# LayerNorm stage of an attention and expert layer: normalising, transposing and copying tile j one tile later, behind the statistics of tile j+1

## The reference

```python
def _layernorm(x, axis=-1, eps=1e-5):
    m = jnp.mean(x, axis=axis, keepdims=True)
    v = jnp.var(x, axis=axis, keepdims=True)
    return (x - m) / jnp.sqrt(v + eps)

xn = _layernorm(x, axis=-1)
x = x + _L0_attn_ref(xn, wq, wkv_a, wkv_b, wo) + _L0_ffn_ref(xn, router_w, gate_w, up_w, down_w)
```

## Time and profile before

| | us |
|---|---|
| two timed executions | 7805.26 and 8367.38, median 8086.32 |
| the profiled execution | 7799.47 |
| its span, slowest core (core 1) | 7797.8 |
| spans of the other cores | 7779.5 to 7793.0 |
| VectorE busy | 2535.1 |
| TensorE busy | 5965.9 |
| ScalarE busy | 818.7 |

### The profile page before, as it was taken

How to read it: one execution, slowest core, us unless ns; L and a number is a source line. 1 busy time by engine, 2 the same in 40 slices (tenths; PEclk the granted TensorE clock), 3 DMA queues, 4 the chain that set the end, 5 groups by cost and what they waited for, 6 DMA issues and landing times.

```text
span 7797.8 us, 77136 instructions; the slowest of 8 cores (7779.5 to 7797.8 us)
## 1 busy us (share of the span) xinstructions
PE 5965.9 (77%) x28992; PEld 2783.4 (36%) x28992; DVE 2535.1 (33%) x4501; ACT 818.7 (10%) x1975; POOL 341.8 (4%) x377
## 2 busy tenths in 40 slices
PE   2655575556555655589999999999999999999900
PEld 1223232223222332234444444444444444444400
DVE  5433343334333433323312332123312332123244
ACT  2011211121111111100000000000000000000000
POOL 0000000000000000000000000000000000000000
PEclk9756575657565756599999999999999999999955
DMA  4200030003000300053243333333243332433166
GB/s 100 28 7 9 7 106 7 9 7 106 7 9 7 105 7 9 1 130 38 28 49 38 38 38 33 44 39 39 27 48 42 39 39 29 49 38 38 24 262 242
DMA packets 509816, 374.91 MB, mean 48 GB/s; under 512 B 468880, under 2 KB 470928, under 8 KB 486928
## 3 DMA queue, kind: packets, MB, share of 16 engines
q0 software_dynamic: 490336, 233.66, 22.4%
q1 hardware_dynamic: 19120, 136.32, 4.5%
HBM read 457.83 MB, written 83.89 MB: 69 GB/s over the span
## 4 chain that ended last, share of the span: by engine, by line
PE 74%; DVE 9%; issue 5%; DMA 4%; DVEq 4%; ACT 3%; ACTq 2%; POOL 0%; POOLq 0%; SPq 0%
PE psG L886 17%; PE psD L909 17%; PE psU L892 17%; PE psA L627 4%; PE psAV L609 4%; PE psA L634 3%; PE psA L555 3%; DMA rb<-scr 3%; PE psTa L600 2%; ACT probs L811 2%; DVEq L713 2%; DVE probsT L734 2%; PE psAV L660 2%; DVE colM L711 2%; PE psA L545 2%
## 5 line engine op out<-in xcount | busy, mean ns | idle before, releaser
L886 PE MATMUL psG<-xnT,gb 128*128 128x512 bf16 x6144 | 1391.5, 380 | 19.4 <-DMA ub<-uw 19.4
L892 PE MATMUL psU<-xnT,ub 128*128 128x512 bf16 x6144 | 1388.7, 379 | 0.0
L909 PE MATMUL psD<-db,hT 128*128 128x512 bf16 x6144 | 1328.6, 379 | 16.6 <-DVE hT L947 16.6
L947 DVE TENSOR_TENSOR hT<-sgt,psU 128x512 bf16<-128x512 f32 x384 | 264.0, 688 | 2409.5 <-PE psU L892 2409.5
L961 DVE SCALAR_TENSOR_TENSOR acc<-psD,comb,acc 128x512 bf16<-128x512 f32 x960 | 720.9, 751 | 541.4 <-PE psD L909 541.4
L886 PEld LDWEIGHTS psG<-xnT,gb 128*128 128x128 bf16 x6144 | 601.7, 98 | 746.7 <-issue 23.5
L909 PEld LDWEIGHTS psD<-db,hT 128*128 128x128 bf16 x6144 | 597.7, 97 | 747.5 <-issue 197.2
L892 PEld LDWEIGHTS psU<-xnT,ub 128*128 128x128 bf16 x6144 | 601.2, 98 | 724.9
L627 PE MATMUL psA<-kns,qn 128*128 128x512 bf16 (+3 forms) x640 | 309.3, 525 | 706.9 <-ACT probs L811 568.8
L934 ACT ACTIVATE sgt<-psG 128x512 f32<-128x512 f32 x384 | 229.4, 597 | 3676.5 <-PE psG L886 3676.5
L811 ACT ACTIVATE probs<-psA,colD 128x512 bf16<-128x512 f32 (+3 forms) x640 | 392.1, 620 | 1669.4 <-DVE colD L714 1475.0
(11 more groups left out here) (135 smaller groups left out, 2842.3 us busy)
## 6 DMA issues: line engine op xcount, KB each, us to landing
scr<-stage SPq DMA_DIRECT2D x64, 1024.0 KB, 3.9
gb<-gw POOLq DMA_DIRECT2D x96, 512.0 KB, 6.5
ub<-uw POOLq DMA_DIRECT2D x96, 512.0 KB, 8.3
db<-dw POOLq DMA_DIRECT2D x16, 3072.0 KB, 20.3
rb<-scr SPq DMA_DIRECT2D x32, 1024.0 KB, 11.7
rb<-scr POOLq DMA_DIRECT2D x32, 1024.0 KB, 10.9
xbuf<-x SPq DMA_DIRECT2D x16, 1024.0 KB, 5.9
xf<-x SPq DMA_DIRECT2D x16, 1024.0 KB, 15.1
```

Of the source, the lines that this page charges most:

```text
L886: i = t.matmul(ps_g[:], gb[sl][:, dc * 128:(dc + 1) * 128], xnt(dc)[:, tb * 512:(tb + 1) * 512], start=(dc == 0), stop=(dc == ND - 1))
L892: i = t.matmul(ps_u[:], ub[sl][:, dc * 128:(dc + 1) * 128], xnt(dc)[:, tb * 512:(tb + 1) * 512], start=(dc == 0), stop=(dc == ND - 1))
L909: i = t.matmul(ps_d[:], hT[:, fc * 2048 + tc * 128: fc * 2048 + (tc + 1) * 128], db[:, fc * 2048 + dcol * 512: fc * 2048 + (dcol + 1) * 51 ...
```

## The change

VectorE's loop is cut into three pieces. The first holds the statistics (L201 to L214) of tile tc. The second, `emit_xnb(j)`, is the wait for `rstd`, the negation and xnb, and marks `xn` and `lnused`. The third, `emit_evac(j)`, is the two copies. In the loop the statistics of tile tc come first, then `emit_xnb(tc - 1)` and `emit_evac(tc - 1)`; behind the loop stand those of the last tile. So that two tiles' values can be kept at once, the columns colC, colD and colE are replaced by pairs in a new tensor `lnc` (mean in columns 0 and 1, variance in 2 and 3, rstd in 4 and 5). One drain goes, that behind the mean of squares. ScalarE's order is kept, with the new columns. SyncE, GpSimd and TensorE have the same programs as before, and `xbuf`, `xnb` and the PSUM tiles have as many buffers as before.

```diff
@@ -123,6 +123,7 @@
                 ivf = EP(nc.sbuf_tensor("ivf", [32, 1], F32))
                 frq = EP(nc.sbuf_tensor("frq", [32, 2048], F32))
                 kfb = EP(nc.sbuf_tensor("kfb", [32, 2048], F32))
+                lnc = EP(nc.sbuf_tensor("lnc", [128, 8], F32))
                 psT0 = EP(nc.psum_tensor("psT0", [128, 1024], BF16))
                 psT1 = EP(nc.psum_tensor("psT1", [128, 1024], BF16))
 
@@ -195,46 +196,59 @@
                     v.drain()
                     VE.inc(i, 1)
                     mark(("cosarg",), VE)
+                    def emit_xnb(j):
+                        wait(v, ("rstd", j))
+                        v.tensor_scalar(out=lnc[:, j % 2:j % 2 + 1], in0=lnc[:, j % 2:j % 2 + 1],
+                                        scalar1=-1.0, scalar2=None, op0=ALU.mult)
+                        v.drain()
+                        i = v.tensor_scalar(out=xnb[:], in0=xbuf[j % 2][:],
+                                            scalar1=lnc[:, j % 2:j % 2 + 1],
+                                            scalar2=lnc[:, 4 + j % 2:5 + j % 2],
+                                            op0=ALU.add, op1=ALU.mult)
+                        v.drain()
+                        VE.inc(i, 1)
+                        mark(("xn", j), VE)
+                        mark(("lnused", j), VE)
+
+                    def emit_evac(j):
+                        for half in range(2):
+                            pt = psT0 if half == 0 else psT1
+                            wait(v, ("xpose", j, half))
+                            dst = xnT[:, half * 8 * 2048: half * 8 * 2048 + 8 * 2048].rearrange(
+                                "p (dc c) -> p dc c", c=2048)[:, :, j * 128:j * 128 + 128]
+                            src = pt[:].rearrange("p (j c) -> p j c", c=128)
+                            i = v.tensor_copy(dst, src)
+                            VE.inc(i, 1)
+                            mark(("xnTevac", j, half), VE)
+
                     for tc in range(NT):
                         wait(v, ("xload", tc))
                         xb = xbuf[tc % 2]
                         v.reduce_sum(colA[:], xb[:], axis=AX.X)
                         v.drain()
-                        v.tensor_scalar(out=colC[:], in0=colA[:], scalar1=float(1.0 / D),
-                                        scalar2=None, op0=ALU.mult)
+                        v.tensor_scalar(out=lnc[:, tc % 2:tc % 2 + 1], in0=colA[:],
+                                        scalar1=float(1.0 / D), scalar2=None, op0=ALU.mult)
                         v.drain()
                         wait(v, ("sq", tc))
-                        v.tensor_scalar(out=colD[:], in0=colB[:], scalar1=float(1.0 / D),
-                                        scalar2=None, op0=ALU.mult)
-                        v.drain()
-                        v.tensor_tensor(out=colA[:], in0=colC[:], in1=colC[:], op=ALU.mult)
-                        v.drain()
-                        v.tensor_tensor(out=colD[:], in0=colD[:], in1=colA[:], op=ALU.subtract)
-                        v.drain()
-                        i = v.tensor_scalar(out=colD[:], in0=colD[:], scalar1=LN_EPS,
+                        v.tensor_scalar(out=lnc[:, 2 + tc % 2:3 + tc % 2], in0=colB[:],
+                                        scalar1=float(1.0 / D), scalar2=None, op0=ALU.mult)
+                        v.tensor_tensor(out=colA[:], in0=lnc[:, tc % 2:tc % 2 + 1],
+                                        in1=lnc[:, tc % 2:tc % 2 + 1], op=ALU.mult)
+                        v.drain()
+                        v.tensor_tensor(out=lnc[:, 2 + tc % 2:3 + tc % 2],
+                                        in0=lnc[:, 2 + tc % 2:3 + tc % 2], in1=colA[:], op=ALU.subtract)
+                        v.drain()
+                        i = v.tensor_scalar(out=lnc[:, 2 + tc % 2:3 + tc % 2],
+                                            in0=lnc[:, 2 + tc % 2:3 + tc % 2], scalar1=LN_EPS,
                                             scalar2=None, op0=ALU.add)
                         v.drain()
                         VE.inc(i, 1)
                         mark(("var", tc), VE)
-                        wait(v, ("rstd", tc))
-                        v.tensor_scalar(out=colC[:], in0=colC[:], scalar1=-1.0,
-                                        scalar2=None, op0=ALU.mult)
-                        v.drain()
-                        i = v.tensor_scalar(out=xnb[:], in0=xb[:], scalar1=colC[:],
-                                            scalar2=colE[:], op0=ALU.add, op1=ALU.mult)
-                        v.drain()
-                        VE.inc(i, 1)
-                        mark(("xn", tc), VE)
-                        mark(("lnused", tc), VE)
-                        for half in range(2):
-                            pt = psT0 if half == 0 else psT1
-                            wait(v, ("xpose", tc, half))
-                            dst = xnT[:, half * 8 * 2048: half * 8 * 2048 + 8 * 2048].rearrange(
-                                "p (dc c) -> p dc c", c=2048)[:, :, tc * 128:tc * 128 + 128]
-                            src = pt[:].rearrange("p (j c) -> p j c", c=128)
-                            i = v.tensor_copy(dst, src)
-                            VE.inc(i, 1)
-                            mark(("xnTevac", tc, half), VE)
+                        if tc >= 1:
+                            emit_xnb(tc - 1)
+                            emit_evac(tc - 1)
+                    emit_xnb(NT - 1)
+                    emit_evac(NT - 1)
 
                 @block.scalar
                 def _(s):
@@ -246,9 +260,10 @@
                         SE.inc(i, 1)
                         mark(("sq", tc), SE)
                         wait(s, ("var", tc))
-                        s.activation(colE[:], colD[:], AF.Ln)
+                        s.activation(lnc[:, 4 + tc % 2:5 + tc % 2], lnc[:, 2 + tc % 2:3 + tc % 2], AF.Ln)
                         s.drain()
-                        i = s.activation(colE[:], colE[:], AF.Exp, scale=-0.5)
+                        i = s.activation(lnc[:, 4 + tc % 2:5 + tc % 2],
+                                         lnc[:, 4 + tc % 2:5 + tc % 2], AF.Exp, scale=-0.5)
                         s.drain()
                         SE.inc(i, 1)
                         mark(("rstd", tc), SE)
```

## The result

| | before | changed |
|---|---|---|
| timed executions | 22, from 7799.16 to 8684.66 us | 23, from 7820.10 to 8641.32 us |
| their median | 7969.36 us | 7939.64 us |
| profiled execution | 7799.47 us | 7823.30 us |
| mean span of the eight cores in it | 7787.5 us | 7813.4 us |
| first key/value matmul, mean of the eight cores | 182.2 us | 202.6 us |

Executions of one and the same program are up to 11% apart here, because in many of them the cores of one die or of both run at a lower clock; the two medians depend on how many of those each kernel drew, and every ratio here leaves them out. The ratio of changed to before is 1.0038, with a 95% interval of 1.0022 to 1.0054: the changed kernel is slower, by 17 to 42 us. The lowest executions of the two kernels are 20.9 us apart. By the bound of 2% the verdict is no change.

The account below looks back on a forecast made before the run. VectorE was taken to bound the LayerNorm stage, whose length goes to the end time. 7799.5 us plus 32.2, mainly from exposed x loads, gave 7831.7, say 7832 us (0.4% more); range 7814 to 7856.

Parts of the forecast that it names:

- the base of the sum: Whole kernel: starting time of 7799.5 us, the profiled execution before (span 7797.8 and 1.7 around it).
- terms of the stage: LayerNorm stage: savings, exposed load, start and end together issue the kvab load 32.2 us later than before.
- The wait for rstd: VectorE before the negation: the wait for ScalarE's Ln and Exp goes, 0.82 us becomes about 0.30, saving 0.52 a tile.
- The drain: VectorE behind the mean of squares: starts 0.08 us apart instead of 0.23, saving 0.15 us, possibly 0.
- The transposes' wait stays: VectorE before the first copy: the 1.37 us wait for TensorE's transposes stays in full.
- The late load: Load of tile j+2, issued behind xnb(j), has 2.83 us but lands after 5.9; pass 11.15 us against 8.58.
- The first pass gains: Start of the LayerNorm stage: one overlapped pass gains 2.5 us, reduce(2) at 36.2 against 38.71.
- The tail: End of the LayerNorm stage: last copy ends at 193.6 us against 159.82 and holds the kvab load, issued at 194.2.
- Every later stage unchanged: Behind the kvab issue: its transfer and every later stage stay unchanged, and nothing of them could start earlier.
- that x loads stay hidden: Rival, LayerNorm stage: loads stay hidden, pass 7.91 us, kvab issued 13 us earlier, 7787 us in total; chance 0.04.
- The longer landing: Rival, x loads: landing takes 9.9 us in every pass, a loss of 88 us, 7888 us in total; chance 0.05.
- The clock: Rival, later stages: TensorE's granted clock shifts, bounded at 6 us; chance 0.10 that later stages move the total over 15 us.

Follow-up runs that it names:

- the late load alone: Kernel before, only SyncE's wait changed: the load of tile tc waits for xnb(tc-1) instead of xnb(tc-2); ratio 1.0035, first matmul at 215.4 us.

## Why the prediction was right or wrong

**The time was wrong.** The measured median is 7939.64 us, and the range ended at 7856. The step that failed is the base of the sum, 7799.5 us from the profiled execution, with the sentence behind it: "The profiled one stands by the lower, and so does this forecast; it is not made against the median". The two executions shown were 7% apart, and I took the higher as something to set aside; the range of 42 us was then built from terms of the stage, and gave 6 us to the spread of executions. What the runs showed in its place: the kernel before has a median of 7969.36 us over 22 executions, 170 us over that base, and the changed one 7939.64 over 23, of which eight are below 7830 us and nine above 8000. No term of the sum stood for that. A forecast of a median has to say how many executions it expects near each of the two values it was shown, and its range has to follow from that.

**That the ratio came out is partly luck.** Against the profiled execution, 7823.30, the forecast of 7832 is 9 us off; as a ratio it was 1.0041, and 1.0038 was measured. But the terms of the stage summed to 32.2 us, and the first matmul moved by 20.4. Of the difference, 5.4 us came from later stages, where the forecast had nothing and where another run shows as much with nothing changed; and the interval of the ratio, 17 to 42 us, holds 20 as well as 32.

**The direction and the mechanism were right.** Point by point:

- *The wait for rstd.* Forecast: 0.30 us from the last statistic to the negation; measured 48.92 to 49.24, 0.32. Right.
- *The drain.* Forecast 0.08 us between the two starts; measured 48.39 to 48.46, 0.07. Right. Reduce to end of xnb: 5.08 us forecast, 5.08 measured (45.73 to 50.81).
- *The transposes' wait stays.* 1.37 us, right.
- *The late load.* Right in kind, and shown by two runs from both sides: three buffers take the loss away, the late load alone makes it. *Its size was the mis-sized term of the stage.* I took a landing of 5.9 us, core 1's median before; on core 3, the slowest after, it was

```profile
DMA to landing us min/median/max: 4.9/5.0/8.9
```

  5.0 us, and 5.0 on core 1 too. The pass shown above is 5.08 + 0.08 + 4.9 + 0.09 = 10.15 (xnb ends at 50.81, issue at 50.89, landing 4.9 later, reduce at 55.88), against a forecast of 11.15. Over 13 passes that would be 13 us. Some passes were longer, up to 11.3 us around 110 us, and the mean pass from tile 2 to tile 15 was (169.96 - 35.55) / 13 = 10.34, so the 13 passes came out 10.5 us shorter than forecast. I held a waiting time fixed that the change itself moved: waiting for a load changes when it is issued, and with that what it meets.
- *The first pass gains.* reduce(2) forecast at 36.2, measured at 35.55 on this core and 36.3 on core 2. Right.
- *The tail.* From the last reduce to the last copy 12.4 us forecast, 12.55 measured. kvab held by the copy, with some 0.6 us of GpSimd's start: 182.51 to 183.20. Right. The transfer itself was forecast at core 1's old 19.9 us; on core 3 it took 18.2 from issue to landing, but on core 3 it had taken 18.8 before, so most of the 1.7 us is a difference of the cores. The rest is open. As a mean of the cores the first matmul is 20.4 us later than before; on this core 20.7.
- *"Every later stage unchanged".* Not shown, and not refuted. The mean span grew by 25.9 us, 5.4 more than the first matmul moved, but the kernel before with a third buffer shows 5.9 us of the same kind with an unmoved stage. Forecast at 32.2, the difference of the spans came out at 25.9.

The rivals: that x loads stay hidden was out after the first look at the waits; but with a third buffer its forecast (7.91 us a pass, 13 us less) is what that kernel did, 7.91 and 12.5. So its arithmetic was right and its condition false. The longer landing didn't come, the opposite did. The clock moved nothing that could be told: 0.93 against 0.94 in the projection, 0.826 as a mean in both, and a part of the chain that ended last of 17% for each of the expert lines as in the earlier trace rows:

```profile
PE psD L924 17%; PE psG L901 17%; PE psU L907 17%; PE psA L642 4%; PE psAV L624 4%; PE psA L649 3%; PE psA L570 3%; DMA rb<-scr 3%; PE psTa L615 2%; PE psAV L675 2%; ACT probs L826 2%; DVEq L728 2%; DVE probsT L749 2%; DVE colM L726 2%; PE 
```

The prediction sets the fit of the Trainium skill ("DMA: Bandwidth & Descriptors", Anatomy of one DMA) against the trace. The page gives that fit for transfers issued from GpSimd. The x loads are issued from SyncE, so their 5.9 us neither bears it out nor refutes it.

## What to carry to other kernels

Before a piece of a loop is moved one iteration later, look for every buffer that it is the last reader of: it keeps that buffer one piece longer, and what refills it is late by as much. Here two buffers were enough with 11.3 us between issue and need, nearly always enough with 6.5, and not with 2.83, at 5 to 6 us of transfer; one more buffer, or releasing the buffer first and doing the statistics of the next tile behind it, turned the same reordering from a loss of 20 us into gains of 12 and 33. Of several waits in a loop, see which one the new order really fills: the larger (1.37 us, the transposes) was untouched until another piece stood between xnb and its copies.

## What the runs showed of the hardware

- One 1 MB load from HBM takes 4.8 to 5.0 us from issue to landing in the best case on these eight cores, and about 6.0 where, as argued above, a neighbour's load meets it. The same figure was 5.2 to 5.9 in medians before, and I had read it as a property of the core.
- Loads that are waited for in each pass settle at about 5.0 us within three passes, but for one load near 110 us, on all eight cores of both kernels that have such waits. Where all loads are hidden and nothing else is loaded, the medians stay at 5.2 to 6.1. A trace of a kernel whose loads are hidden therefore overstates what they would cost once exposed, here by 0.2 to 0.9 us each.
- A 2.3 MB load issued by GpSimd beside x loads of 1 MB stretched x loads to as much as 11.3 us. Where these had 6.5 us from issue to need, VectorE waited 4.9 to 7.3 us in all, at most 4.5 at once; where they had 11.3 or more, not at all.
